# Attention of a fused layer stack: the key's transpose in another PSUM bank, PV first on TensorE, the rounding's last subtraction on VectorE

## The reference

```python
def _div_clamp_fp8(x, scale):
    y = jnp.clip(x.astype(jnp.float32) / scale, -FP8_MAX, FP8_MAX)
    y = y.astype(jnp.bfloat16).astype(jnp.float32)
    return _fp8_roundtrip(y)
...
q = _ln(q, qln_w, qln_b)
k = _ln(k, kln_w, kln_b)
core = _gqa(q, k, v).reshape(b, s, nh * d)
...
cat = jnp.concatenate([core, xout], axis=-1)
catq = _div_clamp_fp8(cat, proj_smooth)
return jnp.einsum('bsi,oi->bso', catq, wproj) * (proj_in_scale * proj_w_scale)
```

## Time and profile before

| | before |
|---|---|
| median of 3 runs (lowest to highest) | 1180.98 us (1179.11 to 1182.12) |
| the profiled execution | 1176.74 us, span 1175.0 us |
| granted TensorE clock, mean of the span | 0.892 |
| PE busy | 903.1 us (77%) |
| DVE busy | 946.7 us (81%) |
| ACT busy | 710.1 us (60%) |
| POOL busy | 394.0 us (34%) |

### The profile page before, as it was taken

One profiled execution on the slowest core, in us unless ns is written; L12 is line 12 of the kernel. 1 busy time (PEld: TensorE's weight loads), 2 busy tenths in 40 slices (PEclk: granted clock), 3 DMA queues, 4 the chain that ended last, 5 costly groups with the idle time before them and its releaser, 6 DMA issues. The chain is left out here.

```text
span 1175.0 us, 23858 instructions
## 1 busy us (share of the span) xinstructions
PE 903.1 (77%) x6878; PEld 781.6 (67%) x6878; DVE 946.7 (81%) x2442; ACT 710.1 (60%) x2471; POOL 394.0 (34%) x498
## 2 busy tenths in 40 slices
PE   3610067423999999999999469999999999998638
PEld 3510033212888888888888358888888888887627
DVE  7989989887888888888888558888888888886461
ACT  3454044374877777777778457667667677674303
POOL 0009900000344444444443443333333433333124
PEclk9965588756999999999999779999999999999559
DMA  6022100002000000000000120000000000000400
GB/s 218 1 108 71 36 1 0 0 0 108 2 1 1 0 0 0 0 0 0 0 0 0 41 86 6 6 7 7 4 4 4 9 4 4 0 0 1 148 19 18
DMA packets 18267, 26.96 MB, mean 23 GB/s; under 512 B 1265, under 2 KB 15409, under 8 KB 17457
## 3 DMA queue, kind: packets, MB, share of 16 engines
q1 hardware_dynamic: 17840, 25.41, 6.3%
q0 software_dynamic: 384, 1.05, 0.3%
HBM read 23.83 MB, written 2.62 MB: 23 GB/s over the span
## 5 line engine op out<-in xcount | busy, mean ns | idle before, releaser
L1392 ACT ACTIVATE c_p<-c_kT_sc_ps,c_nmax 128x64 f32<-128x64 f32 x256 | 76.7, 312 | 72.4 <-DVE c_nmax L1257 72.4
L1213 POOL TENSOR_TENSOR c_cat<-c_tb,c_mb 128x512 fp32r<-128x512 bf16 x64 | 74.4, 1162 | 137.5 <-DVE c_tb L1291 137.5
L1213 POOL TENSOR_TENSOR s_cat<-s_tb,s_mb 128x512 fp32r<-128x512 bf16 x64 | 74.3, 1161 | 116.4 <-DVE s_tb L1291 116.4
L1392 ACT ACTIVATE s_p<-s_kT_sc_ps,s_nmax 128x64 f32<-128x64 f32 x256 | 76.8, 312 | 48.5 <-DVE s_nmax L1257 48.5
L1409 PE MATMUL s_qo_ps<-wq,s_xqf 128*128 128x512 f32 x256 | 71.8, 403 | 32.4 <-POOL s_xqf L1195 32.4
L1409 PE MATMUL c_qo_ps<-wq,c_xqf 128*128 128x512 f32 x256 | 72.1, 404 | 16.4 <-DVE wv L645 16.4
L1473 PE MATMUL c_pj_ps<-wp,c_cat 128*128 128x256 f32 x512 | 78.0, 296 | 1.5 <-POOL c_cat L1213 1.5
L1473 PE MATMUL s_pj_ps<-wp,s_cat 128*128 128x256 f32 x512 | 77.4, 295 | 2.2 <-POOL s_cat L1213 2.2
L1339 DVE TENSOR_TENSOR c_yb<-c_qo_ps,c_ism 128x512 bf16<-128x512 f32 x64 | 44.3, 692 | 43.0 <-PE c_qo_ps L1444 43.0
L1218 POOL TENSOR_TENSOR c_pn<-c_p,c_rsum 128x256 f32<-128x256 f32 x64 | 39.3, 614 | 118.1 <-DVE c_rsum L1346 118.1
L1218 POOL TENSOR_TENSOR s_pn<-s_p,s_rsum 128x256 f32<-128x256 f32 x64 | 39.3, 614 | 106.4 <-DVE s_rsum L1346 106.4
(11 more groups left out here) (359 smaller groups left out, 2889.0 us busy)
## 6 DMA issues: line engine op xcount, KB each, us to landing
x_res<-in_x SPq DMA_DIRECT2D x4, 512.0 KB, 5.8
vT<-in_ctxT SPq DMA_DIRECT2D x2, 1024.0 KB, 10.5
tf_work<-in_wqT SPq DMA_DIRECT2D x2, 1024.0 KB, 6.0
tf_work<-in_wprojT SPq DMA_DIRECT2D x2, 1024.0 KB, 5.5
w_work<-in_wqxT SPq DMA_DIRECT2D x2, 1024.0 KB, 6.5
w_work<-in_wkvxT SPq DMA_DIRECT2D x2, 1024.0 KB, 8.0
c_ctx<-in_ctxT SPq DMA_DIRECT2D x16, 128.0 KB, 2.3
w_work<-in_wprojT SPq DMA_DIRECT2D x2, 1024.0 KB, 5.7
```

The costliest lines, as they stand in the source:

```text
L1213: nc.gpsimd.tensor_tensor(cat[out8.o % 2][:], tb[:], mb[:], ALU.subtract).then_inc(cat_ready, 1)
L1392: nc.scalar.activation(pe_s[:, a * S:(a + 1) * S], sc_ps[:, a * S:(a + 1) * S], ACT.Exp, bias=nmax[:, a:a + 1], accum_out=psum_s[:, a:a + ...
```

## The change

- `kT_ps` moves to columns 256 to 511 of bank 1, and `sc_ps` gets a bank of its own. The key's transposes now wait for the output `yb` (L1339) of two units before instead of the exponentials; the scores wait for the exponentials of the unit before; the transpose of the probabilities waits for `kT` of the unit after (it shares bank 1).
- On TensorE, PV goes to the head of the step, ahead of keys and values; the key's transposes go behind the projection.
- On ScalarE, `kT` goes behind Ln and Exp, and the query's squares go ahead of `pT`.
- On VectorE, `mb` goes between Newton's first and second step, `tb` behind `qn`, and the subtraction `cat` = `tb` - `mb` is done there, between `kn` and `yb`, no longer on GpSimd.

```diff
--- before.py
+++ after.py
@@ -1125,8 +1125,7 @@
 
-        kT_sc_ps = psum("kT_sc_ps", [P, 512])
-        kT_ps, sc_ps = kT_sc_ps[:, 0:KW], kT_sc_ps[:, KW:KW + 4 * S]
+        kT_ps, sc_ps = qo_ps[:, 1, GU * P:GU * P + KW], psum("sc_ps", [P, 512])[:, 0:4 * S]
         pj_ps = psum("pj_ps", [P, 512])
@@ -1206,11 +1205,7 @@
                 def step(i, o):
-                    u, soft, out8 = units(i, o, 0, 1, 3)
-                    if out8.live:
-                        pool.wait_ge(cadd_ready, out8.count(1, 1))
-                        wait_unit(pool, pj_done, out8.before(2))
-                        nc.gpsimd.tensor_tensor(cat[out8.o % 2][:], tb[:], mb[:], ALU.subtract).then_inc(cat_ready, 1)
+                    u, soft = units(i, o, 0, 1)
                     if soft.live:
@@ -1228,7 +1223,7 @@
 
-                pipeline(pool, step, ROUNDS, WIDTH, 3, peel_last=True)
+                pipeline(pool, step, ROUNDS, WIDTH, 1, peel_last=True)
 
@@ -1309,7 +1304,7 @@
                     if f8.live:
-                        for part in range(3):
+                        for part in range(2):
                             round8(part)
@@ -1322,16 +1317,23 @@
                     if u.live:
-                        for part in range(3):
-                            newton(part)
+                        newton(0)
+                    if f8.live:
+                        round8(2)
+                    if u.live:
+                        newton(1)
+                        newton(2)
+                        normalised_query()
                     if f8.live:
                         round8(3)
-                    if u.live:
-                        normalised_query()
                     if sm.live:
...
                         normalised_key()
+                    if f8.live:
+                        dve.wait_ge(cadd_ready, f8.count(1, 1))
+                        wait_unit(dve, pj_done, f8.before(2))
+                        nc.vector.tensor_tensor(cat[f8.o % 2][:], tb[:], mb[:], ALU.subtract).then_inc(cat_ready, 1)
                     if pv.live:
@@ -1366,24 +1368,25 @@
                                              ).then_inc(qT_ready, 1)
-                        act.wait_ge(t_done, sm.count(1, 1))
-                        nc.scalar.activation(kT[:], kT_ps, ACT.Identity, scale=col(f"k{pre}ln_w"),
-                                             bias=col(f"k{pre}ln_b")).then_inc(kT_ready, 1)
                     if u.live:
...
                         nc.scalar.activation(g6[:], l6[:], ACT.Exp, scale=-0.5).then_inc(rs_ready, 1)
+                    if sm.live:
+                        act.wait_ge(t_done, sm.count(1, 1))
+                        nc.scalar.activation(kT[:], kT_ps, ACT.Identity, scale=col(f"k{pre}ln_w"),
+                                             bias=col(f"k{pre}ln_b")).then_inc(kT_ready, 1)
+                    if q.live:
+                        act.wait_ge(q_done, q.count(1, 1))
+                        wait_unit(act, var_ready, q.before(1))
+                        nc.scalar.activation(sq[:, 0:QW], q_bank(q), ACT.Square).then_inc(sqq_ready, 1)
                     if pv.live:
...
                         cross_head_act(act, nc, aw, work, chunks, i, o)
-                    if q.live:
-                        act.wait_ge(q_done, q.count(1, 1))
-                        wait_unit(act, var_ready, q.before(1))
-                        nc.scalar.activation(sq[:, 0:QW], q_bank(q), ACT.Square).then_inc(sqq_ready, 1)
                     if sm.live:
@@ -1413,6 +1416,16 @@
                     u, kv_u, t, pt, pv, pj = units(i, o, 0, 1, 2, 3, 4, 5)
+                    if pv.live:
+                        pe.wait_ge(pT_ready, pv.count(1, 1))
+                        pe.wait_ge(qn_ready, min(pv.n + 3, UNITS) if pv.static else pv.count(1, 3))
+                        for g in range(GU):
+                            for b in range(2):
+                                rows = slice(b * S, (b + 1) * S)
+                                last = nc.tensor.matmul(out_banks(pv)[:, b, g * P:(g + 1) * P],
+                                                        v_s[pv.o % 4][rows, g * D:(g + 1) * D],
+                                                        pT[rows, g * P:(g + 1) * P], start=True, stop=True)
+                        last.then_inc(pv_done, 1)
                     if kv_u.live:
@@ -1435,16 +1448,6 @@
                         last.then_inc(kv_done, 1)
-                    if pv.live:
-                        pe.wait_ge(pT_ready, pv.count(1, 1))
-                        pe.wait_ge(qn_ready, min(pv.n + 3, UNITS) if pv.static else pv.count(1, 3))
-                        for g in range(GU):
-                            for b in range(2):
-                                rows = slice(b * S, (b + 1) * S)
-                                last = nc.tensor.matmul(out_banks(pv)[:, b, g * P:(g + 1) * P],
-                                                        v_s[pv.o % 4][rows, g * D:(g + 1) * D],
-                                                        pT[rows, g * P:(g + 1) * P], start=True, stop=True)
-                        last.then_inc(pv_done, 1)
                     if t.live:
@@ -1454,12 +1457,6 @@
                         last.then_inc(tq_done, 1)
-                        pe.wait_ge(kn_ready, t.count(1, 1))
-                        wait_unit(pe, kT_ready, t.before(1))
-                        wait_unit(pe, exp_ready, t.before(1, 4))
-                        for a in range(GU):
-                            last = nc.tensor.transpose(kT_ps[:, a * P:(a + 1) * P], kn[:, a * P:(a + 1) * P], ident[:])
-                        last.then_inc(t_done, 1)
                     if pj.live:
@@ -1475,6 +1472,13 @@
                         last.then_inc(pj_done, 1)
+                    if t.live:
+                        pe.wait_ge(kn_ready, t.count(1, 1))
+                        wait_unit(pe, kT_ready, t.before(1))
+                        wait_unit(pe, y_ready, t.before(2))
+                        for a in range(GU):
+                            last = nc.tensor.transpose(kT_ps[:, a * P:(a + 1) * P], kn[:, a * P:(a + 1) * P], ident[:])
+                        last.then_inc(t_done, 1)
                     if u.live:
@@ -1486,12 +1490,14 @@
                         wait_unit(pe, y_ready, pt.before(1))
+                        pe.wait_ge(kT_ready, min(pt.n + 2, UNITS) if pt.static else pt.count(1, 2))
                         for g in range(GU):
...
                         pe.wait_ge(kT_ready, t.count(1, 1))
+                        wait_unit(pe, exp_ready, t.before(1, 4))
                         for g in range(GU):
```

## The result

| | before | after |
|---|---|---|
| median (lowest to highest), 4 runs each | 1180.51 us (1179.11 to 1182.12) | 1219.99 us (1218.8 to 1222.62) |
| the profiled execution | 1176.74 us | 1220.58 us, span 1218.9 us |
| mean from sum to sum, self / cross | 5.719 / 6.054 us | 5.947 / 6.511 us |

The ratio is 1.034, with an interval of 1.0315 to 1.0359: slower by 39.5 us. The profiled executions differ by 43.8 us, and the loops hold all of it: 64 units of self 0.228 us longer make 14.6, 64 of cross 0.457 longer make 29.2.

What follows compares the result with a forecast made beforehand. TensorE's work bounds plain cross units, a ring through `qn`, maxima and exponentials self. Cross +24, self +5, loop ends +1 give +30 us: 1207 on the profiled execution, 1211 on the median; range 1187 to 1228.

Steps and rivals of the forecast that it cites:

- The ring of `qn`: `qn`, PV, next unit's keys and values, squares, sum, Newton, `qn`: 6.08 us in plain cross units, 5.61 in self.
- units with the residual: A quarter of all units; forecast 6.87 us for 6.60 in cross (+0.27), 0 in self.
- converting: Units beside which GpSimd converts the next tile, a quarter; forecast +0.51 us in cross, +0.25 in self.
- plain: Units with neither conversion nor residual, half of all; forecast 6.16 us in cross (+0.37), 5.69 in self (+0.03).
- The ring of `kT`: Sum, Exp, late `kT` copy, probabilities' transpose, scores, PV: 3.36 us at PV against 3.25; 0.08 put on plain units.
- The prices beside GpSimd: Instructions stretched in converting units: `mb` up to 0.778 us for 0.294 in cross, the variance 0.51 for 0.17 in self.
- The residual in self: Self units with the residual stand on the old ring as on the new one: change of 0.
- The banks: Key's transposes no longer wait for the previous unit's exponentials: at most some 0.17 us per self unit, where TensorE limits.
- The subtraction: On VectorE between 0.42 and 0.69 us, taken as 0.68, off the ring; cover left 0.4 (self), 0.8 (cross).
- Rival 3: VectorE becomes the limit; if the subtraction also stalls for GpSimd, +38 us, up to 1250; chance 0.10.
- Rival 1: The ring does not close, `qn` being done before TensorE comes to PV: -17 us, 1164; chance 0.08.
- Rival 4: TensorE's clock falls as PE idles in each unit; a tenth of the loops at half speed, +40 us; chance 0.04.

Runs made afterwards that it cites:

- a2: The changed kernel with the key's transposes back ahead of the projection and `kT` back ahead of Ln, PV still first: 1193.87 us, 1.0123.
- a3: The changed kernel with the last subtraction back on GpSimd: 1230.54 us, 1.0423 to the kernel before.
- b3: The kernel before with only the new banks and their waits: 1202.07 us, 1.0162.
- a6: The changed kernel with the subtraction done twice on VectorE, first into a tile nobody reads: 1248.97 us, 1.0587 to the kernel before.
- b1: The kernel before with only PV moved to the head of TensorE's step: 1236.17 us, 1.048.
- n5: The kernel before with VectorE's order changed: `mb` behind Newton's first step, maxima right behind `qn`, then `tb`, `kn`, the residual: 1151.09 us, 0.9743.

## Why the prediction was right, and where it was not

The direction and the range held. The cause is of the kind forecast, a ring on which TensorE's queue stands; the sum was 30 us and it is 39.5 (43.8 on the profiled executions). That the time falls inside the range owes something to the range, which goes up to 1228 for every unit 0.13 us dearer, and to errors of opposite sign, below.

- **The ring of `qn`: right in size, not the one that holds.** a2 has it at 6.02 for 6.08. In after it binds in units with the residual, 6.82 us for the 6.87 forecast, and by 0.13 in the converting ones of cross, but in no plain one. What the prediction named as its sign, idle time before PV put down to `qn` in nearly every cross unit, is not there: 6.7 us in the stage. The other signs came: idle time before the transposes of the probabilities is put down to `kT`, that before the key's transposes is gone, and the sum waits for the squares by 0.6 us in cross.
- **The ring of `kT`: the term that was mis-sized.** I put it 0.08 above the other, so PV at 3.33 behind the sum; it starts at 3.49. The scores hold the queue 1.00 before PV, where I took the 0.81 that they take before keys and values: +0.19. From `kT`'s end to the transposes it is 0.15, not 0.04: +0.11. Transposes to scores 0.25 for 0.22: +0.03. Against that, `kT` starts 0.11 behind Exp's start and not behind its end, and takes 0.55 for 0.60: 1.54 + 0.55 = 2.09 for 1.65 + 0.04 + 0.60 = 2.29, so -0.20. These are 0.13; the other 0.03 is that I used 0.08 where my own sum, PV at 3.36, gave 0.11. Behind PV the way to the next sum took 0.03 more than computed. A plain unit is then 6.35 for 6.16 in cross and 5.87 for 5.69 in self: 0.19 and 0.18 on half of all units, about 12 us. a2 shows the price of `kT` late by experiment: 26 us.
- **By kind of unit, over the whole stages** (each kind's first three left out), the forecast was near in cross (29 us for the 24 forecast) and much too low in self (15 us for 5). Cross: plain +0.53 us for the +0.37 forecast (5.81 to 6.34), converting +0.35 for +0.51, residual +0.32 for +0.27. Self: plain +0.29 for +0.03 (5.62 to 5.91), converting +0.45 for +0.25, residual -0.10 for 0. The plain self units behind a residual take up to 6.01 us and not 5.87; in the one at 522.38 the variance takes 0.29 us beside GpSimd's work. The plain units alone hold the 13 us that the sum of the loops lacked; the errors of the other kinds cancel.
- **The prices beside GpSimd.** In self the variance was stretched as forecast, 0.55 us for 0.17, and the unit is 0.38 above a plain one (forecast 0.34). In cross `mb` was not: GpSimd's long instruction falls on `yb` (L1274, 0.86 us), which costs 0.13 by way of `qn`, and the unit is 6.48 for the 6.65 forecast. The prediction had named that it might shift; a3 shows the dear case, 6.83 to 6.93.
- **The residual in self.** I put it at no change; it is 6.15 us for 6.27, which gives back 2 us.
- **The banks.** The key's transposes stand still no more, as forecast. b3 shows what the prediction did not look at, since in the full change PV first hides it: by themselves they cost 20 us through `yb`.
- **The subtraction.** 683 ns, 64 times in each stage, off the ring, with a little less cover than computed in self (a6). By the 16-bit rule of "VectorE: DVE Perf Modes" in the Trainium skill the upper price was due, and the trace agrees: 683 ns with a 4-byte output, 421 ns for `tb`. Rival 3, VectorE as the limit, did not come: it waits for the squares by 46.2 us in cross, 0.72 per unit. It is near in self, with 7.8 us.
- **Rival 1,** that `qn` comes in time, held in plain units, for another reason than I gave: `kT`'s ring slowed TensorE enough for `qn` to be early. **Rival 4** did not occur in after once the loops were under way (clock 1.00 in every cross unit behind the third, at 92% busy), and did in b1.

The whole, in one line of measured steps: VectorE's order -8 alone, the subtraction -4 alone; with these, the new banks and PV first 1194, +14 to before; `kT` late +26 more. Effects do not add: PV first costs 56 alone (7 of it the clock's), gains 8 where `kT` is early and the new banks are in, and comes out even where `kT` is late.

Left open: why the scores hold the queue for 1.00 before PV and 0.81 to 0.89 before keys and values, what of PE's idle time it took for the clock to fall in b1, and how the gain of n5 divides between the residual and the maxima. None was tried by itself.

## What to carry to other kernels

In a loop that is pipelined by hand, list every ring, a wait on another unit together with all that is queued behind the waiting instruction, and price each in full before moving a step: here, when one was mended or lengthened, the next lay a tenth of a microsecond away. Price it on the mean of each kind of unit and not on one example: in self the one plain unit that was read shows 0.18 us of a miss of 0.25. An instruction moved ahead of others with a wait of its own makes all of them wait; here a wait removed by sharing a bank came back as a wait on the bank's other user. Look first for work that stands ahead of the instruction that the other engines wait for: here the residual and `tb` moved behind the maxima, with `mb` between Newton's steps, were worth 30 us together, with no bank or engine changed.

## What was not expected of the hardware

- An instruction on six numbers per partition took 0.73 us instead of 0.17 because GpSimd had started 0.03 us before it. Between after and a3 GpSimd's start against the sum differs by 0.08 us (1.04 and 0.96 us behind it in the converting units read), and the converting units of cross by 0.4 us. The page "SBUF — State Buffer" of the Trainium skill (section "Who interferes with whom") has GpSimd and VectorE share a pair of ports under a lock; the trace agrees, and shows that the size of the instruction is no shelter.
- In b1 the clock fell in six of the last twelve residual units of cross, each behind an idle time of PE of 1.45 to 1.47 us, and not in the six between them, behind 1.35 to 1.38 us. In the one shown the fall cost 1.2 us (8.61 for 7.40). PE had been busy 94% of the plain unit ahead of it. The waits of 0.25 and 0.41 us in the units of after that are shown left the clock at 1.00.
